# Cross-attention on one core: a PSUM bank for the second Q, held loads at the start, and x of the second tile in one step

## What is computed

```python
q = split(x @ w_q)
k, v = split(text @ w_k), split(text @ w_v)
out_text = merge(softmax(q k^T / sqrt(32)) v)
k_ip, v_ip = split(ip @ w_k_ip), split(ip @ w_v_ip)
out_ip = merge(softmax(q k_ip^T / sqrt(32) + mask_ip) v_ip)
out = (out_text + out_ip) @ w_out + b_out + x
```

## Time and profile before

| | |
|---|---|
| median of three runs | 400.89 us (400.56 to 401.34) |
| the profiled execution | 403.38 us |
| its span, first to last instruction | 401.6 us |
| TensorE busy | 392.8 us (98%) |
| VectorE busy | 339.1 us (84%) |
| GpSimd busy | 154.2 us (38%) |
| ScalarE busy | 129.7 us (32%) |
| DMA, mean | 182 GB/s |
| granted TensorE clock, mean | 0.999 |

### The profile page before, as it was taken

The page is one execution under the profiler, slowest core; times in us unless marked ns, Lnnn a source line. Parts: engine busy times, 40 slices in busy tenths (PEclk is TensorE's granted clock), DMA queues, the critical chain, the costliest instruction groups (busy, mean ns, idle before and its releaser), DMA issues.

```text
span 401.6 us, 10790 instructions
## 1 busy us (share of the span) xinstructions
PE 392.8 (98%) x4452; PEld 291.1 (72%) x4452; DVE 339.1 (84%) x459; ACT 129.7 (32%) x196; POOL 154.2 (38%) x127
## 2 busy tenths in 40 slices
PE   8989999999999999999999999999999999999996
PEld 6778777767777777677777776777777767776775
DVE  4588669989999998899999998998999989989623
ACT  5244333445324322352234322342323322223100
POOL 0057522378526423374226433363226442222200
PEclk9999999999999999999999999999999999999999
DMA  8899926487547544674458445664447554455565
GB/s 285 327 356 365 241 76 176 147 232 217 161 142 230 166 123 128 196 230 130 141 138 257 124 120 155 208 189 138 141 138 247 138 145 125 125 137 147 141 189 194
DMA packets 42993, 72.96 MB, mean 182 GB/s; under 512 B 10560, under 2 KB 10688, under 8 KB 42944
## 3 DMA queue, kind: packets, MB, share of 16 engines
q1 hardware_dynamic: 37824, 67.02, 54.5%
q10 hardware_dynamic: 5120, 5.25, 5.2%
HBM read 35.53 MB, written 10.49 MB: 115 GB/s over the span
## 4 chain that ended last, share of the span: by engine, by line
PE 85%; DMA 5%; DVE 4%; POOL 2%; ACT 1%; SPq 1%; issue 1%; DVEq 0%
PE ps L646 66%; PE ps L695 9%; PE ps L681 8%; DMA stage<-in_x 3%; PE ps L734 2%; DMA x_raw<-in_x 1%; DMA stage<-in_w_out 1%; POOL prob L359 1%; SPq L242 1%; DVE den L530 1%; ACT prob L397 1%; DVE text_max L506 1%; DVE prob L512 1%; DVE prob L523 1%; DVE prob_t L542 0%
## 5 line engine op out<-in xcount | busy, mean ns | idle before, releaser
L359 POOL TENSOR_TENSOR prob<-prob,rden 128x1104 f32<-128x1104 f32 x40 | 82.2, 2055 | 199.0 <-DVE rden L535 199.0
L542 DVE STREAM_TRANSPOSE prob_t<-prob 128x1536 f32<-128x1536 f32 x40 | 70.7, 1767 | 0.1
L397 ACT ACTIVATE prob<-prob 128x1232 f32<-128x1232 f32 x40 | 50.0, 1250 | 59.0 <-DVE prob L523 59.0
L506 DVE TENSOR_REDUCE text_max<-ps 128x16 f32<-128x1104 f32 x40 | 52.2, 1304 | 18.0 <-PE ps L681 17.6
L646 PE MATMUL ps<-x_hi,wq_hi 128*128 128x512 f32 x200 | 59.0, 418 | 1.3 <-ACT q L393 0.7
L646 PEld LDWEIGHTS ps<-x_hi,wq_hi 128*128 128x128 f32 x200 | 34.6, 188 | 34.8 <-issue 27.7
L440 ACT ACTIVATE o_hi<-ps 128x512 fp32r<-128x512 f32 x40 | 23.7, 592 | 101.9 <-PE ps L695 98.1
L646 PE MATMUL ps<-o_hi,wo_hi 128*128 128x512 f32 x200 | 55.8, 392 | 0.6 <-ACT o_hi L440 0.6
L646 PE MATMUL ps<-o_hi,wo_lo 128*128 128x512 f32 x200 | 55.1, 389 | 0.0
L646 PE MATMUL ps<-o_lo,wo_hi 128*128 128x512 f32 x200 | 55.1, 389 | 0.0
L530 DVE TENSOR_REDUCE den<-prob 128x16 f32<-128x1104 f32 x40 | 50.6, 1264 | 4.9 <-ACT prob L397 4.9
(11 more groups left out here) (58 smaller groups left out, 341.3 us busy)
## 6 DMA issues: line engine op xcount, KB each, us to landing
prob_k<-prob_t SPq DMA_DIRECT2D x320, 64.0 KB
stage<-in_x SPq DMA_DIRECT2D x40, 256.0 KB, 3.2
res<-in_x SPq DMA_DIRECT2D x35, 256.0 KB
out_tiles<-res SPq DMA_DIRECT2D x35, 256.0 KB, 2.3
prob_k<-prob_t ACTq DMA_DIRECT2D x160, 32.0 KB
wki_raw<-in_w_k_ip SPq DMA_DIRECT2D x5, 512.0 KB, 7.6
wv_raw<-in_w_v SPq DMA_DIRECT2D x5, 512.0 KB, 8.3
wvi_raw<-in_w_v_ip SPq DMA_DIRECT2D x5, 512.0 KB, 10.3
```

What stands on the lines that cost most here:

```text
L359: nc.gpsimd.tensor_tensor(e[:, :, 0:TEXT], e[:, :, 0:TEXT], rden[:, par, 0, :].unsqueeze(2).to_broadcast([P, QT * HG, TEXT]), ALU.mult)
L397: nc.scalar.activation(prob[:, c % 2, :, 0:TOKENS], prob[:, c % 2, :, 0:TOKENS], ACT.Exp).then_inc(exp_done, 1)
L506: nc.vector.tensor_reduce(text_max[:, par, :, :], s[:, :, :, 0:TEXT], AX_X, ALU.max).then_inc(text_max_done, 1)
L542: nc.vector.transpose(prob_t[:, c % 2, :, :, :].rearrange("p k n r -> p n k r"), prob[:, c % 2, :, :].rearrange("p n (k r) -> p n k r", r= ...
```

## The change

Three edits. Q of unit 1 is written to bank 7, the attention output's, and keys of group 1 move from bank 7 to bank 6. SyncE waits at three places of its prologue until earlier loads have landed: for the first piece of x ahead of w_q of group 1, for the fifth ahead of grid, boxes and identity, and for w_k_ip of group 3 ahead of w_v_ip of group 0; w_v of group 0 and both k weights of group 3 go ahead of that last wait. The five pieces of x of the second tile are all loaded and split in step 1, where three of them were in step 0.

```diff
+FIRST_X_JOBS = {1: (0, 1, 2, 3, 4)}
...
-        K_BANKS = [5, 7, 5, 5, 5]
-        K_PART_BANKS = [6, 7, 5, 5, 5]
+        K_BANKS = [5, 6, 5, 5, 5]
+        K_PART_BANKS = [6, 6, 5, 5, 5]
...
+        def q_bank(c):
+
+            return O_BANK if c == 1 else Q_BANK
...
-            return [("x", first + k) for k in X_JOBS.get(c % KD, ()) if exists(first + k)] + jobs
+            pieces = FIRST_X_JOBS if c < KD else X_JOBS
+            return [("x", first + k) for k in pieces.get(c % KD, ()) if exists(first + k)] + jobs
...
                     sp.dma_start(x0_raw[:, kt, :], x[kt]).then_inc(x0_loaded[kt], 16)
+                sp.wait_ge(x0_loaded[0], 16)
                 load(("w_q", 1))
...
+                sp.wait_ge(x0_loaded[4], 16)
                 sp.dma_start(grid_sb[:, :], grid).then_inc(grid_loaded, 16)
...
                 load_k(2, wki_raw, w_k_ip, wki_loaded)
+                load_v(0, wv_raw, w_v, wv_loaded)
                 load(("w_q", 3))
-                load_v(0, wv_raw, w_v, wv_loaded)
+                load_k(3, wk_raw, w_k, wk_loaded)
+                load_k(3, wki_raw, w_k_ip, wki_loaded)
+                sp.wait_ge(wki_loaded[1], 32)
                 load_v(0, wvi_raw, w_v_ip, wvi_loaded)
                 load(("w_q", 4))
-                load_k(3, wk_raw, w_k, wk_loaded)
-                load_k(3, wki_raw, w_k_ip, wki_loaded)
                 load_v(1, wv_raw, w_v, wv_loaded)
                 load_v(1, wvi_raw, w_v_ip, wvi_loaded)
...
-                nc.scalar.activation(q[:, c % 2, :], ps[:, Q_BANK, :], ACT.Copy, scale=SCALE).then_inc(q_copied, 1)
+                nc.scalar.activation(q[:, c % 2, :], ps[:, q_bank(c), :], ACT.Copy, scale=SCALE).then_inc(q_copied, 1)
...
                     if n == 0:
-                        if c >= 1:
+                        if c >= 2:
                             pe.wait_ge(q_copied, c)
...
-                    last = product(Q_BANK, wq_hi, wq_lo, x_hi, x_lo, b, g, n, c > 0)
+                    last = product(q_bank(c), wq_hi, wq_lo, x_hi, x_lo, b, g, n, c > 0)
...
+                if g == 1:
+                    pe.wait_ge(k_part_copied, 1)
                 if g >= 2:
                     pe.wait_ge(k_copied, g if g > 2 else 1)
```

## The result

The changed kernel takes 408.12 us, median of six runs (406.54 to 409.82), against 400.73 us (399.33 to 401.34) of the kernel before. The ratio is 1.019 (95% interval 1.0158 to 1.0223): slower by 7.4 us. The forecast was 403.8, range 399.0 to 405.6: the sign was right, the size was not.

A forecast was written before the change was run, and what follows sets the result against it. TensorE bounds the kernel (85% of the chain), through its waits in the first 50 us. Late x +1.4 and clock +1.5 make +2.9 us: 403.38 becomes 406.3, less 2.49 to the median gives 403.8, range 399.0 to 405.6.

The forecast's parts named there:

- The bank: Q of unit 1 may start at 10.46 in bank 7; gain 0.8 us, less if w_k_ip comes later; key group 1: nothing.
- the first two holds: SyncE's early loads go back by 1 and 2 us, hidden by queue backlog: costed at nothing, ends -0.6 and +0.6 us.
- the third hold as a gain: w_k of group 3 lands at 28.0, TensorE's wait for it goes, TensorE is 2.4 us ahead; other end leaves 0.8 us.
- The first fold of v: Loads behind the third hold: w_v_ip 0 lands 31.9, needed about 33.8; w_k 4 36.3 to 38.2, needed about 38.6: covered.
- The last x: Last x of the second tile lands at 50.0, not 48.6; TensorE goes on at 51.05 against 49.63: +1.4 us.
- The clock: After TensorE stands still 5.2 us ahead of the fold of v of group 1, its clock falls: 1.5 us, ends 0 and 2.6.
- the last one: Converting profile to median: profiled 403.38 becomes 406.3; the median was 2.49 us below the profiled execution, so 403.8.
- Quicker landings with fewer in flight: Rival: last x lands at 46.2, TensorE goes on at 47.3, clock unaffected: -2.4 us, 398.5; chance 0.22.
- The clock holds: Rival: last x late as forecast, but TensorE's clock doesn't fall, so without the 1.5 us: 402.3; chance 0.20.
- the two cancel: Rival: last x lands at 48 to 49 us and the clock holds or nearly: 400.9; chance 0.13.

The follow-up runs named there:

- The filled gap: The changed kernel plus 24 matmuls of 128x512 into empty bank 7 ahead of the second fold of v, results unused: 408.14 us, ratio 1.0173.
- second profile of before: The kernel before, without an edit, profiled once more: one execution of 401.31 us, span 399.5.
- late x_hi on the changed kernel: The changed kernel with ScalarE making the five x_hi of step 1 in step 2, behind the copy of Q: 405.96 us, ratio 1.0136.

## Why the prediction was right in sign and wrong in size

**The bank, the first two holds, the third hold as a gain: right.** Q of unit 1 began at 10.27 (10.5 forecast), keys of group 3 at 27.93 (28.0) with no wait, the hold ended at 28.79 (28.3), w_v_ip landed at 28.79 + 3.6 = 32.4 (31.9). The first two holds cost nothing, also alone.

**The first fold of v: missed.** The prediction asked whether w_v_ip 0 and w_k 4 would be there in time, but not w_q of group 4, which also stands behind the hold. ScalarE waited for it until 33.27, issued its four moves, the copy of the image part came at 36.47, and TensorE lost 1.37 us. This had no price of its own, since TensorE only came later to the wait of step 2 (46.19 + 4 x 0.235 = 47.13, counted as the prediction does; 45.8 was forecast).

**The last x: right mechanism, size off.** Forecast 50.0, by 294 KB/us, with 51.4 at 273 KB/us as the other end. The fifth x_hi began at 51.67, right behind the fourth, so the last x had landed by then; from 32.4 that is 5312 KB in at most 19.3 us, 275 KB/us. The fourth piece has a landing on record, 51.12: 5056 KB in 18.7 us, 270 KB/us. The choice of the faster of the two rates was the wrong one, by up to 1.2 us, and the later landing of w_v_ip, 0.5 us, is the rest. TensorE went on at 52.69 in place of 51.05: +3.06 us and not +1.4 to the profiled execution of before.

**The clock: right, 0.4 us short.** It fell after the rest and took 1.94 us (5.11 - 3.17) where 1.5 was forecast. The filled gap shows the same stretch at full clock in 3.19 us; that its whole time is no shorter (408.14) leaves open what the fall costs at the end.

By these steps the sum was +1.4 + 1.5 = +2.9; it came to 3.06 + 1.94 = +5.0 at the first attention output. In the spans it is +4.0. The prediction let every microsecond at 50 us come out at the end, but 0.9 of the 5.0 go between 80 and 90 us: the step there, in which the first profile of before has its wait of 0.57 us for o_hi, takes 8.89 us before and 7.99 after.

**The step that failed most is the last one**: "403.38 us for its span of 401.6; it becomes 406.3. The median of the runs was 400.89, 2.49 us below it, so 403.8." The 2.49 us are no offset that the changed kernel inherits, as far as three profiled executions can tell. That of before happened to have a late last x (48.60; 47.30 when run again), a late w_k (1.4 us of wait; 0.4) and the late piece of w_out at 84.65. These make the 2.1 us between the two spans of before, 1.3 and 0.9, and in the changed kernel none of them is left: the change puts the end of the same queue at 51.67 by its own means, there is no wait for o_hi, and its profiled execution lies 0.7 us below its median, not 2.5 above it. Against the second profile of before the account closes: the fold of v is 4.4 us later (52.69 against 48.33), the clock takes 1.9, and the spans differ by 6.1; with the 0.7 that the profile after lies below its median and the 0.6 that this one of before lies above its own, that is the 7.4 between the medians. The 4.3 us between 403.8 and 408.1 are these: 1.1 in the spans (4.0 against 2.9), 2.5 from this step, 0.7 from where the profiled execution after lies. Without the step the forecast would have been 406.3.

**What was not seen at all** is that the order of the loads has a price by itself. Moving 832 KB (w_v_ip 0 and w_q 4) behind the wait for a k slot empties the queue at 22 to 24 us, and that alone cost 2.0 to 2.9 us. The count of kilobytes from the end of the hold took both holes in without knowing it. Roughly it fits: two windows of 2 us at 38 and 14 GB/s where 408 and 363 were moved leave out 0.74 + 0.70 = 1.44 MB, which is 4 us at 360 GB/s, and against the second profile of before the last x_hi is 51.67 - 47.30 = 4.4 us later. It is an estimate: the windows around the two differ as well, both ways.

**The rivals.** "Quicker landings with fewer in flight" was half right: w_k 3, with one load behind it, took 3.4 us where it had taken 6.7, and w_v_ip 0, the first into the empty queue, 3.6. The Trainium skill, page "DMA: Bandwidth & Descriptors", section "Latency and other measured facts", says that a lighter load makes a transfer's fixed cost smaller; the landings agree with the direction, though they can't tell a fixed cost from the time that other loads' bytes take. But the queue lost more by being empty than each load gained. "The clock holds" and "the two cancel" are out. Of the signs that the prediction named all of the right ones came (no wait for wk_raw, Q at 10.3, a hole at 28 to 30 us, the last x_hi after 50, one gap of over 4 us with a low clock behind it).

**What stays open.** Why the loss is not additive: x in step 1 costs 1.8 us alone, the order 2.0 to 2.9, the hold in the old order 5.2 to 7.0, hold and order 7.3, and all together 7.4. A late queue reaches TensorE at one fold or at the other, and one of them pays; this is argued and was not tested. Nor is it known how the changed kernel loses 5.5 us when the gap before the second fold is taken away; the late moves of probabilities and the fallen clock were seen, not varied. Nor was it found why the change without the third hold costs 4.9 us where its parts, the order (at most 2.9) and bank with x in step 1 (0.7), make at most 3.6. That profile has a gap of 4.6 us with the lower clock behind it, and two late causes that meet in one gap would do this.

## What to carry to other kernels

Before adding a wait to a queue, or moving a load behind one, ask what is still in flight while it stands: where nothing is, the engines of the transfers run empty (38 and 14 GB/s here), and where that queue is behind until a late consumer, the lost time comes out at its end. The kilobytes still to come from that point, at the slower of the rates the trace shows, gave the landing here. An in-order engine that waits for a transfer ahead of a small copy that TensorE needs passes such lateness on, and so does its own work there; put the copy first. Here that was worth 0.25 to 0.39% together with the bank, and nothing that the runs can tell from noise alone. And a profile is one execution: a landing that the change takes over should be compared with the median's, not have the profile's distance to the median carried along.

## What was unexpected of the hardware

- The clock fell after a rest of 1.45 us (late x_hi on the changed kernel, 0.54 in the window of 38 to 40 us), while rests of 1.43 us, 1.94 and 2.0 us passed at 1.00. By these runs the length of one rest does not decide alone.
- In the changed kernel the clock fell during the 5.30 us rest, at 50 us, and was at the lower level for about 7 us, some 4 of them after TensorE was busy again at 52.69; that stretch of work took 1.9 us longer. After the 1.45 us rest it fell only when TensorE was at work again: the window of 36 to 38 us, with the rest in it, shows 1.00.
- The same last x was there for ScalarE at 48.6 and at 47.3 us in two executions of the same kernel, and ten runs of the kernel with the new order alone spread from 401.2 to 407.6 us, with mean clocks from 1.000 down to 0.990: when an x is late the clock may fall as well, or not.
